# Attention scores of an AdaLN-attention-FFN block, computed in 64-row tiles of the array

## The reference

```python
# cond: one 32x32 matrix per sequence, applied over the token axis
c = einsum('bct,bcd->bdt', x, weights[subjects])
# attention, 32 heads of 16 channels, rope, causal softmax
q, k, v = proj(wq), proj(wk), proj(wv)        # from c; each (b, 32 heads, 32 tokens, 16)
q, k = rope(q), rope(k)
scores = einsum('bnth,bnsh->bnts', q, k) / sqrt(16)
out = einsum('bnts,bnsh->bnth', softmax(where(causal, scores, -inf)), v)
x = x + out @ wo.T
# base linear + top-2 of 8 LoRA experts, then a 16-headed FFN on permuted channels
t = x @ W.T + 2 * sum_e gates_e * (x @ A_e.T) @ B_e.T
x = x + unpermute(down(gelu(up(permute(t)))))
```

## Time and profile before

| | us |
|---|---|
| median of 3 runs | 293.57 (293.10 to 294.01) |
| profiled execution | 292.91 |
| its span, first to last instruction | 291.1 |
| TensorE matmuls busy | 257.2 |
| VectorE busy | 173.6 |
| ScalarE busy | 139.2 |
| GpSimd busy | 107.7 |

### The profile page before, as it was taken

How to read it: one execution, slowest core, us unless ns; L and a number is a source line. 1 busy time by engine, 2 the same in 40 slices (tenths; PEclk the granted TensorE clock), 3 DMA queues, 4 the chain that set the end, 5 groups by cost and what they waited for, 6 DMA issues and landing times.

```text
span 291.1 us, 5710 instructions
## 1 busy us (share of the span) xinstructions
PE 257.2 (88%) x2293; PEld 207.6 (71%) x2304; DVE 173.6 (60%) x356; ACT 139.2 (48%) x276; POOL 107.7 (37%) x82
## 2 busy tenths in 40 slices
PE   0799398999999999999999999999989964789895
PEld 0689396778766788779776977797759743458764
DVE  0556379998598868464169583741677814335402
ACT  1342364237672336975322359953113597921460
POOL 2636379649840502157806011668060111100000
PEclk9999879999999999999999999999999999999999
DMA  4599603000000000012000000010000000001001
GB/s 127 148 345 254 145 12 134 0 2 1 2 0 2 5 0 2 0 62 84 2 0 2 0 2 2 2 74 0 0 2 2 0 2 0 3 0 73 0 2 72
DMA packets 13498, 11.42 MB, mean 39 GB/s; under 512 B 7576, under 2 KB 9368, under 8 KB 13472
## 3 DMA queue, kind: packets, MB, share of 16 engines
q1 hardware_dynamic: 12608, 9.85, 11.2%
q0 software_dynamic: 576, 1.18, 1.5%
q10 hardware_dynamic: 288, 0.03, 0.1%
HBM read 8.96 MB, written 2.10 MB: 38 GB/s over the span
## 4 chain that ended last, share of the span: by engine, by line
PE 67%; ACT 9%; DVE 9%; DMA 5%; issue 4%; SPq 4%; POOL 1%; ACTq 0%; DVEq 0%
PE ps_D L435 7%; ACT pbd L809 6%; PE ps_A L435 6%; PE ps_S L503 6%; PE ps_A L436 5%; PE ps_A L437 5%; PE ps_D L437 5%; PE ps_D L436 5%; PE ps_C L518 5%; PE ps_D L628 4%; PE ps_C L435 4%; PE ps_C L437 4%; PE ps_C L436 4%; SPq L325 3%; DMA pbd<-in_L_ffn_perm 2%
## 5 line engine op out<-in xcount | busy, mean ns | idle before, releaser
L809 ACT ACTIVATE pbd<-pr 32x256 f32<-32x256 f32 x128 | 53.0, 414 | 14.2 <-PE ps_C L518 7.3
L390 POOL TENSOR_TENSOR kbd<-kr,cst 128x1024 f32<-128x1024 f32 x16 | 35.2, 2221 | 29.1 <-PE ps_S L503 29.1
L399 POOL TENSOR_TENSOR pr<-pr,small 128x512 f32<-128x512 f32 x16 | 16.5, 1049 | 59.8 <-DVE small L1065 59.8
L377 POOL TENSOR_TENSOR rot<-rot,cst 128x512 f32<-128x512 f32 x16 | 20.7, 1292 | 32.4 <-DVE rot L1030 32.3
L873 ACT ACTIVATE act<-ps_D 128x512 f32<-128x512 f32 x32 | 19.0, 598 | 13.1 <-PE ps_D L437 11.5
L518 PE MATMUL ps_C<-pbd,vz 128*32 128x128 f32 x512 | 20.0, 278 | 5.4 <-ACT pbd L809 5.2
L1041 DVE TENSOR_TENSOR kbd<-kr,cst 128x1024 f32<-128x1024 f32 x16 | 24.6, 1555 | 0.0
L435 PE MATMUL ps_A<-xc,wkT 128*128 128x256 f32 x64 | 19.5, 305 | 4.6 <-DVE qr L1031 4.6
L518 PEld LDWEIGHTS ps_C<-pbd,vz 128*32 128x32 f32 x512 | 12.3, 109 | 13.3 <-ACT pbd L809 7.8
L435 PE MATMUL ps_D<-y,upP 128*128 128x256 f32 x64 | 19.6, 305 | 0.8 <-DVE y L997 0.8
L997 DVE TENSOR_TENSOR y<-ps_S,y 128x512 fp32r<-128x512 f32 x8 | 5.4, 677 | 24.7 <-ACT y L809 24.7
(11 more groups left out here) (186 smaller groups left out, 698.5 us busy)
## 6 DMA issues: line engine op xcount, KB each, us to landing
xs<-in_x SPq DMA_DIRECT2D x4, 512.0 KB, 3.9
out<-xs SPq DMA_DIRECT2D x3, 512.0 KB, 2.8
pbd<-in_L_attn_wq SPq DMA_DIRECT2D x2, 512.0 KB, 6.2
act<-in_L_attn_wk SPq DMA_DIRECT2D x1, 1024.0 KB
pr<-in_L_attn_wv SPq DMA_DIRECT2D x1, 1024.0 KB, 9.0
xs<-in_L_attn_wo SPq DMA_DIRECT2D x1, 1024.0 KB
out<-xs SPq DMA_DIRECT2D x2, 256.0 KB, 2.0
pbd<-in_L_cond_A SPq DMA_DIRECT2D x1, 256.0 KB
```

Source lines behind the costliest of these rows:

```text
L377: pool.tensor_tensor(rv, rv, con("sin").unsqueeze(1).to_broadcast([P, 2 * N // T, T]), ALU.mult).then_inc(rot_sin, 1)
L390: pool.tensor_tensor(kbd[:, c, :, :].rearrange("p b (h s) -> p b h s", h=HC), kv.unsqueeze(2).to_broadcast([P, BT, HC, T]), con("head").un ...
L399: pool.tensor_tensor(pr[:, i, :, :], pr[:, i, :, :], mx[:, i, :].unsqueeze(2).to_broadcast([P, NH // 2, T]), ALU.mult).then_inc(normed, 1)
L809: return sc.activation(dst, src, ACT.Copy)
```

## The change

Each chunk of 128 channels (8 heads) is cut into two halves of 64 channels, 4 heads each. Row half r works on rows 64r to 64r + 63 of the array and writes bank r of ring S. The host lays the rows of wq and wk out so that in each chunk the first 64 channels are heads 4c to 4c + 3 and the last 64 are heads 16 + 4c to 16 + 4c + 3; bank 0 still holds heads 0 to 15 and bank 1 heads 16 to 31. `kbd` has room for 4 heads instead of 8 per channel, so `k_blocks` writes 128x512 instead of 128x1024. A call of `scores(g, t)` now fills both banks of a token tile: both masks first, then per chunk 4 sequences x 2 halves, each 64 rows, 32 columns, 128 streamed columns. Both banks are signalled full at the end of the last chunk. `scored` counts three chunks of a tile instead of every even chunk.

In TensorE's order `experts_base(g-1, 0)` moves ahead of the second tile's scores, and the second tile's second half, which stood behind `experts_lora`, is no longer apart. On VectorE `max_shift(g, 1)` and the key block of chunk 2 (`k_blocks(g, 1, 2)`) move ahead of `logits_out(g-1)` and of `gates`.

```diff
-for _name, _n in [("ident", P), ("cos", T), ("sin", T), ("causal", T), ("head", HC), ("seq", BT),
+for _name, _n in [("ident", P), ("cos", T), ("sin", T), ("causal", T), ("head", HG), ("seq", BT),
...
-    put("head", (p // HD)[:, None] == np.arange(HC)[None])
+    put("head", (p // HD % HG)[:, None] == np.arange(HG)[None])
...
-        kbd = sb("kbd", [P, KC, BT, HC * T])
+        kbd = sb("kbd", [P, KC, BT, HG * T])
...
         def wait_scored(eng, n):
-            if n % 2:
-                wait_full(eng, S_scores(n // 8, n // 2 % 4))
+            tile, c = n // KC, n % KC
+            if c == KC - 1:
+                wait_full(eng, S_scores(tile // GT, 2 * (tile % GT) + 1))
             else:
-                eng.wait_ge(scored, n // 2 + 1)
+                eng.wait_ge(scored, (KC - 1) * tile + c + 1)
...
-            def scores(g, i):
-                t, half = i // 2, i % 2
-                it = S_scores(g, i)
-                wait_free(pe, it)
-                if g == 0 and i == 0:
+            def scores(g, t):
+                its = [S_scores(g, 2 * t + r) for r in range(2)]
+                if g == 0 and t == 0:
                     pe.wait_ge(mask_ready, 2)
-                pe.matmul(bank(it)[:, :], ident_b[:, :], mask_b[:, :, :].rearrange("p h s -> p (h s)"),
-                          start=True, stop=False, skip_group_check=True)
+                for it in its:
+                    wait_free(pe, it)
+                    pe.matmul(bank(it)[:, :], ident_b[:, :], mask_b[:, :, :].rearrange("p h s -> p (h s)"),
+                              start=True, stop=False, skip_group_check=True)
                 pe.wait_ge(roped, 4 * g + 4)
-                for c in (2 * half, 2 * half + 1):
+                for c in range(KC):
                     n = 8 * g + 4 * t + c
                     pe.wait_ge((kbd_v, kbd_p)[c % 2], n // 2 + 1)
                     for b in range(BT):
                         at = P * t + T * b
-                        last = pe.matmul(bank(it)[T * b:T * b + T, N * (c % 2):N * (c % 2) + N],
-                                         qr[:, c, at:at + T], kbd[:, c, b, :], start=False, stop=True,
-                                         skip_group_check=True)
-                    last.then_inc(scored if c % 2 == 0 else s_full(it), 1)
+                        for r in range(2):
+                            rows = slice(P // 2 * r, P // 2 * r + P // 2)
+                            last = pe.matmul(bank(its[r])[T * b:T * b + T, P * c:P * c + P],
+                                             qr[rows, c, at:at + T], kbd[rows, c, b, :], start=False, stop=True,
+                                             skip_group_check=True)
+                            if c == KC - 1 and b == BT - 1:
+                                last.then_inc(s_full(its[r]), 1)
+                    if c < KC - 1:
+                        last.then_inc(scored, 1)
...
                     scores(g, 0)
-                    scores(g, 1)
                     lora_down(g - 1)
                     turn_logits(g - 1)
-                scores(g, 2)
+                    experts_base(g - 1, 0)
+                scores(g, 1)
                 if g:
-                    for c in range(KC - 1):
+                    for c in range(1, KC - 1):
                         experts_base(g - 1, c)
...
                     experts_lora(g - 1, 1)
-                scores(g, 3)
...
                 max_shift(g, 0)
                 k_blocks(g, 1, 0)
+                max_shift(g, 1)
+                k_blocks(g, 1, 2)
                 if g:
                     logits_out(g - 1)
-                max_shift(g, 1)
                 if g == 0:
-                    k_blocks(0, 1, 2)
...
                     gate_h(g - 1)
-                    k_blocks(g, 1, 2)
...
+    rows = np.array([(16 * r + 4 * c + h) * HD + d for c in range(KC) for r in range(2) for h in range(HG)
+                     for d in range(HD)])
     for name in _INS:
-        give(f"in_{name}", inputs[name])
+        a = inputs[name]
+        give(f"in_{name}", a[rows] if name in ("L0_attn_wq", "L0_attn_wk") else a)
```

More of the change, by code:

```diff
@@ L40 @@
 HC = P // HD
+HG = HC // 2
 XS = 3
@@ L390, in k_blocks @@
                 pool.tensor_tensor(
-                    kbd[:, c, :, :].rearrange("p b (h s) -> p b h s", h=HC),
-                    kv.unsqueeze(2).to_broadcast([P, BT, HC, T]),
-                    con("head").unsqueeze(1).unsqueeze(3).to_broadcast([P, BT, HC, T]),
+                    kbd[:, c, :, :].rearrange("p b (h s) -> p b h s", h=HG),
+                    kv.unsqueeze(2).to_broadcast([P, BT, HG, T]),
+                    con("head").unsqueeze(1).unsqueeze(3).to_broadcast([P, BT, HG, T]),
                     ALU.mult).then_inc(kbd_p, 1)
@@ L694, in _ @@
             scores(0, 0)
-            scores(0, 1)
             prep_ar()
```

## The result

The change was slower. Its first four executions had a median of 296.98 us against 293.75 us of before: a ratio of 1.012, 95% interval 1.009 to 1.015. The forecast was 292.6 us, a little faster. Timed again later, twelve executions had a median of 295.11 (292.99 to 298.10) against 293.59: ratio 1.004, interval 1.001 to 1.007. The ratio leaves out the execution of 298.10, which was over 1.5% above the fastest of the twelve. Both timings are slower, by different amounts, and the spread of the change is itself a result: 5.1 us, 3.8 without the longest, where before spread over 2.3 us on that chip.

A forecast was written before the change was run, and what follows sets the result against it. TensorE, busy 88% of the span, was taken to bound the kernel, with ScalarE setting the pace from 232 to 262 us. Group 0's -1.6 and groups 1 to 3's +0.6 gave -1.0 us, a median of 292.6; range 290.5 to 297.0.

The forecast's parts named there:

- the first rival: Scores on TensorE: 64-row tiles do not overlap, a tile saves 0.20 us, total +5.5, about 299 us; chance 0.20.
- a forecast 1.58: Scores on TensorE: one tile would cost 1.58 us instead of 2.66, a saving of 1.08.
- The gain of group 0: Group 0, which has neither new wait: reaches the end of its softmax work 1.6 us earlier.
- Both new waits: TensorE in groups 1 to 3: 1.45 us more at the logits' transposes and 0.9 before the first FFN product.
- rounds of 0.14 us: Score rounds on TensorE, estimated from the skill page: 0.14 us instead of 0.11, making the sum about 2 us worse.
- the sum for groups 1 to 3: Groups 1 to 3: -2.16 from tiles, +1.45 and +0.9 from waits, +0.19 us each, +0.6 together.
- The wait at the logits: TensorE before the logits' transposes, waiting for VectorE's late copy: 1.45 us, bounds 1.25 and 2.0.
- dearer waits: Rival: key blocks disturbed by GpSimd (+1.7 us) or partial row overlap (+1.3): 293.5 to 295.5 us; chance 0.20.
- The wait before the FFN: TensorE between last LoRA product and first FFN product, hand-over of x2 uncovered: 0.9 us, bounds 0.8 and 1.0.
- my -1.0: Whole kernel: -1.6 us from group 0 and +0.6 from groups 1 to 3, -1.0 in total.
- the faster that led my chances: Whole kernel: below 292.7 us counts as faster; chance 0.39, against 0.35 same and 0.26 slower.
- I count no change of clock.: TensorE's granted clock: taken as 1.00, the 2.4 GHz level, throughout, so no time was counted for a change.

The follow-up runs named there:

- the third profile: The unaltered change, a single execution profiled later: 293.78 us, no half clock between 60 and 230 us.
- the three later ones: The three later timings of the unaltered kernel before, 42 executions; means of 293.02, 293.57 and 293.98 us over similar clocks.
- the first profile: The unaltered change, the profiled execution of its first timing, slowest of four: 298.17 us, span 296.4 us.
- the early copy: The change with VectorE's copy of the logits put back ahead of the second shift and second key block: 289.42 us, ratio 0.987 against before.
- the first expert block ahead: The change with the first expert block moved ahead of the logits' transposes in TensorE's queue: 290.73 us, ratio 0.990 against before.
- the experiment that filled the wait: The change with the first expert block computed once more ahead of the logits' transposes, then overwritten: 296.25 us, ratio 1.008 against before.

## Why the prediction was wrong

**What held.** The 64-row tiles overlap; the first rival, no overlap, is out. A tile cost 1.67 us for a forecast 1.58. The gain of group 0 was 1.63 us for 1.6. Both new waits came where they were placed, released by the engine and the instruction named. The last 59.9 us kept their length in an execution without falls there. Key blocks of 0.68 (VectorE, alone) and 1.07 us (GpSimd) are as expected. The Trainium skill ("TensorE: Matmul & The Clock Gate", Part 3) gives a measured speedup of 3.07 for four tiles that split the array's rows; the estimate made from it in the prediction was rounds of 0.14 us. The run gives 0.11 from round to round, and that decides.

**What failed first: the sum for groups 1 to 3**, "+0.19 each, +0.6 together". Without any fall each costs +1.0 us (21.14 - 20.16, 21.15 - 20.17, 20.25 - 19.25), +3.0 together. Four terms make the 0.8:
- The wait at the logits was sized 1.45 and measured 1.84 by the same reckoning. From the start of the product the transposes came 4.72 us later in the change (92.08 to 96.80) and 2.88 in before: 1.84. Of the 0.4 too little, 0.26 is the first key block beside GpSimd's: 0.86 us of VectorE's time instead of 0.6, the bound I had priced under dearer waits. 0.09 is the signal to TensorE, 0.15 instead of 0.06. And 0.14 I took off twice: the 2.88 held the ordinary step already, so it was not to be subtracted again. Against that, VectorE started 0.05 after TensorE left the scores, not 0.14.
- A tile saves 2.66 - 1.67 = 0.99 instead of 1.08: 0.2 in two tiles.
- The wait before the FFN is 108.61 to 109.67, 1.06 from last product to next, near the 1.08 of the row I had; less the ordinary step that is 0.95, and I took 0.9.
- The rest, about 0.15, I can't place with certainty. The second tile now stands between two expert blocks, and the first fp32r product behind fp32 tiles takes 0.22 to its successor instead of 0.12.

So an undisturbed change would have been 2.4 us above my -1.0: about +1.4 by this sum, +0.8 in the third profile (span 291.9 against 291.1, in which the start before the first mask gave back 0.6). That is between 0.3 and 0.5%, and not the faster that led my chances.

**What failed second: "I count no change of clock."** At mean clocks of 0.985 or more the change took 293.97 us in the second timing and before 293.02 in the three later ones, a difference of 0.9 us, near the 0.8 of the third profile; what lies above that comes mostly with lower clocks. "1.00 throughout" was also misread: before's own trace has 0.50 for 6.8 us at 33.7 us, in the start, and 1.00 only from there on. Between 60 and 230 us TensorE never idled over 0.9 us in before. The change adds three idle stretches of 1.74 us there, and a fall after one costs 1.5 us. I had worked out these waits and priced them as waits only. In the first profile the falls in groups 1 and 2 are 3.0 of the 5.3 us of span (22.62 + 22.66 against 21.14 + 21.15). The waits less the gain of the tiles are 1.3, the rest between groups 0.1, and 1.2 came from half clock at 248.5 us in the last stretch; the start gave back 0.3. The 1.2 is not put down to the change: the early copy and the first expert block ahead have half clock there too, and they are fast.

**The numbers.** The range, up to 297.0, just held 296.98, by luck: for a reason that was in none of the cases, and with the wrong sign. Slower had 0.26, of which 0.20 was on tiles that do not overlap. The case that came, waits that eat the gain and then the clock, was not among the rivals. The nearest, dearer waits, ended at 295.5, which is where the second timing lies.

**Where the expected gain went** is shown by undoing the order. The same 64-row tiles with nearly the old order around them give -2.2%, 7 us. The reordering, made to let both banks fill at once, cost all of that and 1.5 to 3 us more. That the falls come from the idleness rests on the count, 6 behind 21 waits and none at 18 places without; the experiment that filled the wait did not settle it. What stays open is the time of that kernel, which by its middle should have been as fast as the change without falls, and the part of the first timing that the clock does not explain.

## What to carry to other kernels

When a change makes an early engine faster, look first at every instruction whose place on the other engines moves with it: here a copy of 0.41 us that slipped behind three instructions cost 5 to 7 us, most of what eight score tiles gained. Price a new wait on TensorE twice, once as idleness and once as the risk that the work after it runs at half clock. And a hand-over that another piece of work covered is paid in full when that piece is made shorter or moved; put the shortened piece back over it.

## What the hardware showed that was not expected

- TensorE's granted clock fell to 0.50 for 3.4 us after 6 of 21 idle stretches of 1.73 to 2.29 us, within 1.7 us of their end, while it was busy again, and after none of 18 places with less idleness; the same wait in the same kernel was followed by a fall in one execution and not in the next.
- Eight 64x32 tiles in fp32 run side by side: 64 records in 1.16 us, in rounds of eight 0.11 us apart, where 16 of double length took 1.07. With the same matmuls ordered half by half it is 1.56, and the second half's first matmuls start 0.3 us before the first half's last.
- VectorE's 128x512 key block takes 0.68 us alone and 0.94 when it begins 0.4 us before the end of one of GpSimd's of the same size.
